# Cross-attention on one core: where seven of 16 transposed context tiles land in PSUM, in what order they are issued, and which slots split self-attention's weights

## The chip, the cores and the metric

The kernel runs on one core of a Trainium2 chip. The metric is the device time of one execution in microseconds (us), the median of the runs of one kernel. TensorE (PE), VectorE (DVE), ScalarE (ACT), GpSimd (POOL) and the DMA queue of SyncE (SP) each follow a list of instructions of their own and meet at semaphores.

## The reference, cut to what matters

```python
x = x + xattn(layernorm(x), ctx)      # x 4 x 128 x 512, ctx 4 x 2048 x 512, 16 heads of 32
x = x + self_attn(layernorm(x))       # 4 x 128 tokens, rotary, 16 heads
x = x + moe(layernorm(x))             # 8 experts, top 2, hidden 1024
# xattn:
cn = layer_norm(ctx, g2, b2)
k, v = cn @ Wk.T, cn @ Wv.T
out = softmax(q @ k.T / sqrt(32) + mask) @ v
return out @ Wo.T + bo
```

The change lies in the cross-attention, and in the preparation of self-attention's weights that is done beside it.

## The kernel before, in words

**Windows and slots.** The cross-attention goes through 16 windows, w = 4b + g, for batch b and a group g of four heads. A window has eight slots, p = 0 to 7, and a slot takes two tiles of 128 keys. `window_steps` (L57) writes the order of the steps of a window out by hand; `all_steps` (L154) puts the windows in a row behind a set-up, and every engine runs through the same list and takes its own part of each step. Only DVE's list is changed a little by `halves_behind_maxima` (L163): the subtraction of a block of keys is put behind the next two maxima or tiles.

**The steps of a slot.** PE has one long block per slot, in four pieces between which the other steps stand. Slot 0 is the last keys block of window w + 1 (`k`, L799), slots 1 to 4 are its four blocks of values (`v`, L815), and slots 5 to 7 are the first three blocks of keys of window w + 2. Around them stand:

- `s` (L854): the scores of the next slot, into `ps_s`; ACT takes the exponential of them (L694), POOL adds that to a running sum (L430).
- `av` (L869): the slot's probabilities times values.
- `p1` (L832): one of 16 products of queries and keys of window w + 1, of which DVE takes the maximum (L536). `MAXIMA_AT` (L52) says how many a slot holds: 2, 4, 4, 3 and 3 in slots 2 to 6. `mt` (L849) turns the maxima into a row.
- `st`, `nm`: DVE's statistics and normalisation of the next batch's context tiles, in windows with g below 3.
- `t` (L779), only in the windows with g = 2 of batches 0 to 2 (w = 2, 6 and 10, the turning windows): 16 context tiles of the next batch are transposed, four 128x128 transposes each. ACT copies the high half out of the bank (L630), DVE writes the rest as a low half (L524), and only then is the bank free. `TURNING_AT` (L54) gives the order of tiles and maxima in each slot, here `tptptp` in slots 2 to 5, `tptp` in 6 and `tt` in 7. The first four of a slot's such steps go between the four pieces of the long block, the fifth and the sixth behind it, ahead of `av`.
- `den`, `low`, `op`, `wo`: the end of the window before, and the output projection.

**Banks.** Two rings of two PSUM banks each serve these steps. Ring a (`ps_a`, `bank_a_free` L715) is for the blocks of keys and values and the output projection; of its two banks one is being filled while the one before is emptied by ACT. Ring b (`ps_b`, `bank_b_free` L728) is for `t`, `p1` and `mt`, which take its two banks in turn in the order of the steps. PE waits ahead of a step until the bank's last user has been read: for a `t` on DVE's low half (`tr_lo`), for a `p1` on its maximum (`p1_max`), for a block on ACT's copy (`k_f_out`, `v_out`).

**Self-attention's weights.** When the context tiles of the last batch are transposed, the four weights of self-attention are loaded into their place (`self_weight_in`, L315) as 16 pieces of 128x512. Each is split into two halves, `spl`: ACT writes the high half (L710), waiting for the low half of the piece before, and DVE then the low half (L586), waiting for ACT. `SPLITS_AT` (L53) puts five pieces into each of windows 11, 12 and 13 and the last into window 14: one in slot 0, two in slot 1, two in slot 7, all behind the third piece of the long block. Nothing in the cross-attention waits for them.

SP follows the same list. At every fourth `t` it waits until the tile is transposed and issues the next 1 MB load; at the second and the fourth block of keys it moves 12 parts of the halves into `k_stack`. After the 16 windows come self-attention and the mixture of experts, which the change does not touch.

Of the kernel before, what the change touches and what calls it, by code (L numbers as in the profile page):

```python
# [14 lines left out]
ALU, ACT, AX = mybir.AluOpType, mybir.ActivationFunctionType, mybir.AxisListType  # L15
# [36 lines left out]
MAXIMA_AT = {2: 2, 3: 4, 4: 4, 5: 3, 6: 3}  # L52
SPLITS_AT = {0: (0,), 1: (1, 2), 7: (3, 4)}  # L53
TURNING_AT = ("", "ppp", "tptptp", "tptptp", "tptptp", "tptptp", "tptp", "tt")  # L54


def window_steps(w):  # L57
# [11 lines left out]
    for p in range(NPAIR):  # L69
# [103 lines left out]


NORMED = ((0, NB - 1), (NB - 1, NB))

# [12 lines left out]
def cross_attention(nc, io, t, s):  # L189


    steps = all_steps("PE")
    ring_a = [step[:3] for step in steps if step[0] in ("k", "v", "op") and step[-1] == 0]
    ring_b = [step for step in steps if step[0] in ("t", "p1", "mt")]
    ring_a = [(step[0], step[1]) if step[0] == "op" else step for step in ring_a]
    KIN = 16 * 3 * HPG
# [6 lines left out]
    with ExitStack() as ctx:  # L203
# [94 lines left out]

        def bank_a(step):
            return ps_a[ring_a.index(step) % 2]  # L300

        def bank_b(step):
            return ps_b[ring_b.index(step) % 2]

# [137 lines left out]
        def _(v):  # L442
# [58 lines left out]
            for step in all_steps("DVE"):  # L501
# [19 lines left out]
                elif kind == "t":  # L521
                    b, kt = step[1:]
                    v.wait_ge(tr_hi, NKT * b + kt + 1)
                    nc.vector.tensor_tensor(cT_lo[:, :, P * kt:P * (kt + 1)],  # L524
                                            bank_b(step)[:, :].rearrange("p (c n) -> p c n", c=NC),
                                            cT_hi[:, :, P * kt:P * (kt + 1)], ALU.subtract).then_inc(tr_lo, 1)
# [6 lines left out]
                elif kind == "p1":  # L533
                    w, j, kb = step[1:]
                    v.wait_ge(p1_mm, nth_p1(step))
                    nc.vector.tensor_reduce(mpart[:, j, kb:kb + 1], bank_b(step)[:, :], AX.X, ALU.max).then_inc(p1_max, 1)  # L536
                    if (j, kb) == (HPG - 1, NKB - 1):
# [15 lines left out]
                elif kind == "op" and step[2] == NG - 1:  # L553
                    b = step[1]
                    v.wait_ge(op_mm, b + 1)
                    nc.vector.scalar_tensor_tensor(out=t.x[:, b, :], in0=bank_a(step[:2])[:, :], scalar=UNSCALE,
                                                   in1=t.x[:, b, :], op0=ALU.mult, op1=ALU.add).then_inc(x_done, 1)
# [17 lines left out]
                elif kind == "xln":  # L575
                    v.wait_ge(x_done, NB - 1)
                    for b in range(NB - 1):
                        nc.vector.bn_stats(t.a_stats[:, b, :], t.x[:, b, :]).then_inc(s.a_st, 1)
                    v.wait_ge(s.a_st, NB - 1)
                    for b in range(NB - 1):  # L580
                        last = nc.vector.bn_aggr(t.a_mv[:, b, :], t.a_stats[:, b, :])
                    last.then_inc(s.a_var, 1)
                elif kind == "spl":
                    n = step[1]
                    v.wait_ge(s.self_hi, n + 1)
                    nc.vector.scalar_tensor_tensor(out=self_weight(n, "lo"), in0=self_weight(n, "raw"),  # L586
                                                   scalar=W_SCALE, in1=self_weight(n, "hi"), op0=ALU.mult,
                                                   op1=ALU.subtract).then_inc(s.self_lo, 1)

        @block.scalar  # L590
        def _(act):
# [33 lines left out]
            for step in all_steps("ACT"):  # L625
                kind = step[0]
                if kind == "t":
                    b, kt = step[1:]
                    act.wait_ge(tr, NKT * b + kt + 1)
                    nc.scalar.activation(cT_hi[:, :, P * kt:P * (kt + 1)],  # L630
                                         bank_b(step)[:, :].rearrange("p (c n) -> p c n", c=NC),
                                         ACT.Copy).then_inc(tr_hi, 1)
# [13 lines left out]
                elif kind == "v" and step[3] == QUAD - 1:  # L646
                    w, q = step[1:3]
                    act.wait_ge(v_mm, NQ * w + q + 1)
                    if w == 0 and q == 0:
                        act.wait_ge(w_lo, 3)  # L650
                    nc.scalar.activation(vals[w % 2][:, QUAD * q:QUAD * (q + 1), :].rearrange("p k n -> p (k n)"),
                                         bank_a(step[:3])[:, :], ACT.Copy, scale=UNSCALE).then_inc(v_out, 1)
                elif kind == "k" and step[3] == NC - 1:
# [6 lines left out]
                    else:  # L660
                        act.wait_ge(q_lo_s, NG)
                    nc.scalar.activation(k_f[:, kb % 2, :], bank_a(step[:3])[:, :], ACT.Identity,
                                         bias=kbias[:, g:g + 1], scale=UNSCALE).then_inc(k_f_out, 1)
# [12 lines left out]
                elif kind == "mt":  # L676
# [4 lines left out]
                        t.q_stack[SHIFT_ROW:SHIFT_ROW + 1, HPG * g:HPG * (g + 1), b * P:(b + 1) * P],  # L681
                        bank_b(step)[SHIFT_ROW:SHIFT_ROW + 1, :].rearrange("o (j n) -> o j n", j=HPG),
                        ACT.Copy, scale=-1.0).then_inc(m_row, 1)
# [17 lines left out]
                elif kind == "wo":  # L701
                    c = step[1]
                    act.wait_ge(w_in[3], 16)
                    nc.scalar.activation(wo_hi[:, c, :], folded[3][1][:, c, :], ACT.Copy, scale=W_SCALE).then_inc(w_hi, 1)
                elif kind == "spl":
                    n = step[1]
# [7 lines left out]
        def _(pe):  # L714
            def bank_a_free(step):  # L715

                at = ring_a.index(step)
                if at >= 2:
                    before = ring_a[at - 2]
                    if before[0] == "k":  # L720
                        pe.wait_ge(k_f_out, NKB * before[1] + before[2] + 1)
                    elif before[0] == "v":
                        pe.wait_ge(v_out, NQ * before[1] + before[2] + 1)
                    else:
                        pe.wait_ge(x_done, before[1] + 1)
                return ps_a[at % 2]

            def bank_b_free(step):  # L728

                at = ring_b.index(step)  # L730
                if at >= 2:
                    before = ring_b[at - 2]
                    if before[0] == "t":
                        pe.wait_ge(tr_lo, NKT * before[1] + before[2] + 1)
                    elif before[0] == "p1":
                        pe.wait_ge(p1_max, nth_p1(before))
                    else:
                        pe.wait_ge(m_row, before[1] + 1)
                return ps_b[at % 2]

# [36 lines left out]
            for step in steps:  # L777
                kind = step[0]
                if kind == "t":  # L779
                    b, kt = step[1:]  # L780
                    bank = bank_b_free(step)
                    pe.wait_ge(normed, NKT * b + kt + 1)
# [16 lines left out]
                elif kind == "k":  # L799
                    w, kb, c = step[1:]  # L800
                    b, g = w // NG, w % NG
                    if c == 0:
                        bank_a_free(step[:3])
# [4 lines left out]
                    bank, col, keys = bank_a(step[:3]), slice(P * g, P * (g + 1)), slice(KB * kb, KB * (kb + 1))  # L808
                    nc.tensor.matmul(bank[:, :], t.wk_hi[:, c, col], cT_hi[:, c, keys], start=(c == 0), stop=False)  # L809
# [5 lines left out]
                elif kind == "v":  # L815
                    w, q, i = step[1:]
                    b, g = w // NG, w % NG
                    if i == 0:
                        bank_a_free(step[:3])
# [5 lines left out]
                    to, keys = bank_a(step[:3])[:, P * i:P * (i + 1)], slice(P * kt, P * (kt + 1))  # L825
                    for c in range(NC):
# [5 lines left out]
                elif kind == "p1":  # L832
                    w, j, kb = step[1:]
                    b, g = w // NG, w % NG
                    bank = bank_b_free(step)
                    if (j, kb) == (0, 0):
# [9 lines left out]
                elif kind == "mt":  # L846
                    w = step[1]
                    bank = bank_b_free(step)
                    pe.wait_ge(m_max, w + 1)  # L849
# [48 lines left out]
                elif kind == "op":  # L898
                    b, g = step[1:]
                    if g == 0:  # L900
                        bank_a_free(step[:2])
                        pe.wait_ge(w_lo, 3 + NC)
                    to = bank_a(step[:2])
                    pe.wait_ge(split_lo, NG * b + g + 1)
# [1070 lines left out]
```

## Time and profile before

| | us |
|---|---|
| runs | 1005.8, 1005.98, 1001.48 |
| median | 1005.8 |
| the profiled execution, its own time | 1000.39 |
| its span in the trace | 998.6 |
| mean granted TensorE clock in it | 0.959 of full speed |

The profiled execution is one more run. Its own time is 1.8 us above its span, and it lies 5.4 us below the median of the three. In the trace the windows' stage goes from 98 to about 664 us; in it the shown duration of a matmul is longer than the distance to the next, so times on PE are read here from start to start. A slot is measured from the start of one `av` (L879) to the start of the next.

### The profile page before, as it was taken

Reading aid. Unit: us, or ns where it says so; the run is one execution under the profiler, and the core shown is the slowest. Engines: PE = TensorE matmul, PEld = TensorE weight load, DVE = VectorE, ACT = ScalarE, POOL = GpSimd, SP = SyncE. Lnnn points to the kernel's source line nnn. Section 1 sums busy time; section 2 is a strip of 40 time slices with the busy share of each in tenths; the row PEclk is TensorE's granted clock in tenths of the full one; section 3 lists DMA queues with packets and bytes.
Section 4 is the critical chain, followed back from the end, with each engine's and each line's share of the span. In section 5 each row is a group of like instructions: output and inputs, shape, how many; then the busy total and the mean of one; then the engine's idle time right before and its main releaser. Section 6 shows DMA issues by size and latency. Waiting matters only on the chain. (4 is left out here: it accounts for less than half of the span.)

```text
span 998.6 us, 24592 instructions
## 1 busy us (share of the span) xinstructions
PE 908.0 (91%) x10413; PEld 609.7 (61%) x10413; DVE 687.8 (69%) x1024; ACT 529.6 (53%) x813; POOL 385.4 (39%) x290
## 2 busy tenths in 40 slices
PE   5998999999999999999999999996876669999996
PEld 2463775765765766766757657663444367777773
DVE  7764787646777645688546656665687757999993
ACT  3643345555344453444464544551376447999993
POOL 2130665344566435556435444452230132112112
PEclk9997999999999999999999999998897778999998
DMA  9362121352121332221332201216502727999993
GB/s 341 103 182 57 34 65 43 107 148 71 41 65 34 113 107 55 60 54 26 94 117 77 66 20 47 59 30 252 192 2 84 283 84 268 397 404 401 402 359 48
DMA packets 48456, 134.64 MB, mean 135 GB/s; under 512 B 9870, under 2 KB 11790, under 8 KB 44506
## 3 DMA queue, kind: packets, MB, share of 16 engines
q1 hardware_dynamic: 45356, 126.78, 37.6%
q0 software_dynamic: 2800, 6.04, 3.0%
q8 instruction: 83, 1.36, 0.6%
q10 hardware_dynamic: 192, 0.26, 0.1%
q14 instruction: 25, 0.20, 0.1%
HBM read 94.99 MB, written 11.33 MB: 106 GB/s over the span
## 5 line engine op out<-in xcount | busy, mean ns | idle before, releaser
L430 POOL TENSOR_TENSOR acc_pool<-acc_pool,pT 128x1024 f32<-128x1024 f32 x90 | 211.5, 2350 | 162.6 <-ACT pT L694 161.0
L536 DVE TENSOR_REDUCE mpart<-ps_b 128x1 f32<-128x512 f32 x256 | 174.0, 686 | 87.4 <-PE ps_b L843 86.5
L694 ACT ACTIVATE pT<-ps_s 128x1024 f32<-128x1024 f32 x124 | 126.5, 1021 | 199.3 <-PE ps_s L865 199.3
L827 PE MATMUL ps_a<-wv_hi,cT_hi 128*128 128x128 f16 x1024 | 184.3, 220 | 0.4 <-ACT kbias L611 0.4
L829 PE MATMUL ps_a<-wv_hi,cT_lo 128*128 128x128 f16 x1024 | 183.2, 219 | 0.0
L828 PE MATMUL ps_a<-wv_lo,cT_hi 128*128 128x128 f16 x1024 | 183.1, 219 | 0.0
L827 PEld LDWEIGHTS ps_a<-wv_hi,cT_hi 128*128 128x128 f16 x1024 | 99.8, 97 | 12.4 <-issue 11.9
L843 PE MATMUL ps_b<-k_stack,q_stack 98*128 98x512 f16 x256 | 98.0, 386 | 9.4 <-DVE mpart L536 5.4
L828 PEld LDWEIGHTS ps_a<-wv_lo,cT_hi 128*128 128x128 f16 x1024 | 100.2, 98 | 5.0
L531 DVE TENSOR_TENSOR k_lo<-k_f,k_hi 128x512 f16<-128x512 f32 x64 | 67.9, 1061 | 48.9 <-ACT k_hi L667 48.5
L829 PEld LDWEIGHTS ps_a<-wv_hi,cT_lo 128*128 128x128 f16 x1024 | 99.8, 97 | 0.0
L809 PE MATMUL ps_a<-cT_hi,wk_hi 128*128 128x512 f16 x256 | 98.3, 384 | 0.0
L865 PE MATMUL ps_s<-q_stack,k_stack 98*128 98x128 f16 x992 | 93.4, 220 | 5.3 <-ACT pT L694 4.3
L810 PE MATMUL ps_a<-cT_lo,wk_hi 128*128 128x512 f16 x256 | 97.3, 380 | 0.0
L811 PE MATMUL ps_a<-cT_hi,wk_lo 128*128 128x512 f16 x256 | 97.1, 379 | 0.0
L865 PEld LDWEIGHTS ps_s<-q_stack,k_stack 98*128 98x128 f16 x992 | 70.7, 98 | 40.9 <-ACT pT L694 11.0
L1846 PE MATMUL ps_h<-m_xT_hi,cT_hi 128*128 128x128 f16 x480 | 82.6, 221 | 2.4 <-issue 1.5
L1552 POOL DMA_INDIRECT out<-x_sb,rows_in x15 | 31.7, 2114 | 136.5 <-DMA out<-x_sb,rows_in 115.9
L879 PE MATMUL ps_o<-pT,vals 128*32 128x128 f32 x2048 | 82.4, 278 | 1.3 <-ACT pT L694 1.3
L1848 PE MATMUL ps_h<-m_xT_hi,cT_lo 128*128 128x128 f16 x480 | 82.5, 221 | 1.0 <-issue 1.0
L1847 PE MATMUL ps_h<-m_xT_lo,cT_hi 128*128 128x128 f16 x480 | 82.5, 221 | 0.1
L524 DVE TENSOR_TENSOR cT_lo<-ps_b,cT_hi 128x512 f16<-128x512 f32 x64 | 43.8, 689 | 52.7 <-ACT cT_hi L630 52.7
(255 smaller groups left out, 1877.7 us busy)
## 6 DMA issues: line engine op xcount, KB each, us to landing
w_raw<-in_w SPq DMA_DIRECT2D x30, 2048.0 KB, 12.9
raw<-in_context SPq DMA_DIRECT2D x16, 1024.0 KB, 5.8
k_stack<-k_hi SPq DMA_DIRECT2D x252, 64.0 KB, 2.0
k_stack<-k_lo SPq DMA_DIRECT2D x128, 64.0 KB, 2.0
slots_in<-a_zeros SPq DMA_DIRECT2D x1, 3855.0 KB, 12.8
rows_in<-slots_in SPq DMA_DIRECT2D x15, 257.0 KB, 11.6
q_stack<-k_stack SPq DMA_DIRECT2D x12, 128.0 KB, 2.3
x_sb<-in_x SPq DMA_DIRECT2D x2, 512.0 KB, 4.3
```

The lines of the kernel that those rows point to most:

```text
L430: nc.gpsimd.tensor_tensor(acc_pool[:, :], pT[:, 0, :] if p == 1 else acc_pool[:, :], pT[:, p % PT, :], ALU.add).then_inc(pool_add, 1)
L536: nc.vector.tensor_reduce(mpart[:, j, kb:kb + 1], bank_b(step)[:, :], AX.X, ALU.max).then_inc(p1_max, 1)
L694: nc.scalar.activation(pT[:, p % PT, :], scores(w, p)[:, :], ACT.Exp, scale=SM_SCALE).then_inc(exp_done, 1)
L809: nc.tensor.matmul(bank[:, :], t.wk_hi[:, c, col], cT_hi[:, c, keys], start=(c == 0), stop=False)
L810: nc.tensor.matmul(bank[:, :], t.wk_hi[:, c, col], cT_lo[:, c, keys], start=False, stop=False)
L811: last = nc.tensor.matmul(bank[:, :], t.wk_lo[:, c, col], cT_hi[:, c, keys], start=False, stop=(c == NC - 1))
L827: nc.tensor.matmul(to, cT_hi[:, c, keys], t.wv_hi[:, c, col], start=(c == 0), stop=False)
L828: nc.tensor.matmul(to, cT_hi[:, c, keys], t.wv_lo[:, c, col], start=False, stop=False)
L829: last = nc.tensor.matmul(to, cT_lo[:, c, keys], t.wv_hi[:, c, col], start=False, stop=(c == NC - 1))
L843: nc.tensor.matmul(bank[:, :], t.q_stack[0:ROWS, HPG * g + j, b * P:(b + 1) * P], t.k_stack[w % 2][0:ROWS, j, KB * kb:KB * (kb + 1)], star ...
L865: last = nc.tensor.matmul(scores(w, p)[:, at:at + P], t.k_stack[w % 2][0:ROWS, j, P * kt:P * (kt + 1)], t.q_stack[0:ROWS, HPG * g + j, b * ...
L1846: nc.tensor.matmul(to, w1_hi[u][:, c, col], xT_hi[u][:, c, :], start=(c == 0), stop=False)
```

## The change

Four things are edited. (1) Seven of the 16 tiles of batches 1 to 3, those in `ASIDE`, go into a bank of ring a instead of ring b: the one whose turn comes next, while the current block fills the other. The other nine tiles, the `p1` and the `mt` keep ring b. `banks_of` notes for each use its bank and the use before it in that bank, and PE waits for that. (2) The order of tiles and maxima in the turning windows' slots 3, 4 and 6 is another. (3) In a slot, a fifth such step stands behind `den`, `low` and `op`, right ahead of `av`, and a sixth behind `av`. (4) Self-attention's pieces: one a slot, in the same windows; ACT's high half is in slots 1 to 5, DVE's low half one slot later, in 2 to 6, behind the slot's second maximum.

```diff
-SPLITS_AT = {0: (0,), 1: (1, 2), 7: (3, 4)}
-TURNING_AT = ("", "ppp", "tptptp", "tptptp", "tptptp", "tptptp", "tptp", "tt")
+TURNING_AT = ("", "ppp", "tptptp", "ttppt", "tptppt", "tptptp", "tpptp", "tt")
+
+ASIDE = (0, 4, 6, 7, 10, 12, 15)
...
-        behind = [("spl", 5 * (w - 11) + n) for n in SPLITS_AT.get(p, ()) if 11 <= w and 5 * (w - 11) + n < 4 * NC]
...
-        for n in range(max(4, len(side))):
+        low, high = [[("spl" + part, 5 * (w - 11) + q - 2)] if w >= 11 and 2 <= q <= 6 and 5 * (w - 11) + q - 2 < 4 * NC
+                     else [] for part, q in (("_lo", p), ("_hi", p + 1))]
+        for n in range(4):
             steps += heavy[n:n + 1] + side[n:n + 1]
             if n == 1:
-                steps += nxt[:1] + light[:1]
+                steps += nxt[:1] + low + light[:1]
             if n == 2:
-                steps += nxt[1:] + light[1:] + behind
+                steps += nxt[1:] + high + light[1:]
+        late = [side[4:5], side[5:6]]
...
-        steps += [("av", w, p, 0), ("av", w, p, 1)]
+        steps += late[0] + [("av", w, p, 0), ("av", w, p, 1)] + late[1]
...
+def banks_of(steps):
+
+    begun, last, place = {"a": 0, "b": 0}, {}, {}
+    for step in steps:
+        kind = step[0]
+        use = step[:2] if kind == "op" else step[:3]
+        if kind in ("k", "v", "op"):
+            if use in place:
+                continue
+            bank = ("a", begun["a"] % 2)
+            begun["a"] += 1
+        elif kind == "t" and step[1] and step[2] in ASIDE:
+            bank = ("a", begun["a"] % 2)
+        elif kind in ("t", "p1", "mt"):
+            use = step
+            bank = ("b", begun["b"] % 2)
+            begun["b"] += 1
+        else:
+            continue
+        place[use] = (bank, last.get(bank))
+        last[bank] = use
+    return place
...
-            def bank_b_free(step):
-
-                at = ring_b.index(step)
-                if at >= 2:
-                    before = ring_b[at - 2]
-                    if before[0] == "t":
-                        pe.wait_ge(tr_lo, NKT * before[1] + before[2] + 1)
...
+            def bank_free(use):
+
+                before = banks[use][1]
+                if before is not None and before[0] == "k":
+                    pe.wait_ge(k_f_out, NKB * before[1] + before[2] + 1)
...
+                elif before is not None and before[0] == "t":
+                    pe.wait_ge(tr_lo, NKT * before[1] + before[2] + 1)
...
+                return bank_at(use)
```

The order of PE in slots 2 to 6 of a turning window after the change, with V and K for a piece of the long block, t for a tile, t* for a tile in ring a, p for a maximum's product and s for scores:

```
slot 2   V t0* V p s V t1  s V p      t2  av
slot 3 p V t3  V t4* s V p s V p      t5  av
slot 4   V t6* V p s V t7* s V p      p   av
slot 5 t8 K t9 K p s K t10* s K p     t11 av
slot 6 p K t12* K p s K p  s K        t13 av
```

Slot 7 has `mt`, t14 and t15*. The step ahead of slot 3, 5 and 6 is the sixth of the slot before.

## Rows read from the trace of the kernel before

**Rows 1.** The page: busy time of the engines over the span.

```profile
PE 908.0 (91%) x10413; PEld 609.7 (61%) x10413; DVE 687.8 (69%) x1024; ACT 529.6 (53%) x813; POOL 385.4 (39%) x290
```

**Rows 2.** Windows view: stretch, length, busy us of PE, PEld, DVE, ACT, POOL, clock.

```profile
137.37:141.59 4.22, 4.22 (x82) 3.68 (x73) 4.14 (x11) 1.67 (x4) 3.48 (x4) 1.00 0.34 81
141.59:146.28 4.69, 4.69 (x79) 3.86 (x77) 3.42 (x10) 1.74 (x3) 2.78 (x4) 1.00 0.29 70
150.96:155.34 4.38, 4.38 (x41) 2.20 (x40) 3.32 (x9) 1.28 (x3) 2.49 (x2) 1.00 0.00 0
173.92:180.31 6.39, 6.09 (x95) 5.01 (x86) 4.48 (x8) 3.83 (x8) 2.99 (x2) 1.00 0.38 92
193.16:199.50 6.34, 6.02 (x53) 3.50 (x52) 3.87 (x6) 3.23 (x6) 2.35 (x2) 1.00 0.34 130
...
173.92:204.92 31.00, 29.46 (x365) 21.38 (x356) 19.83 (x34) 15.75 (x27) 11.76 (x5) 1.00 0.39 122
482.62:513.64 31.02, 29.48 (x366) 21.40 (x358) 19.84 (x34) 15.77 (x27) 11.78 (x5) 1.00 0.38 118
...
399.48:403.75 4.27, 4.27 (x46) 2.27 (x45) 1.29 (x2) 2.77 (x4) 0.30 (x1) 1.00 0.44 110
531.41:537.17 5.76, 4.85 (x78) 3.86 (x76) 4.99 (x9) 2.82 (x5) 2.35 (x1) 1.00 0.21 51
554.95:560.72 5.77, 4.34 (x45) 2.27 (x44) 2.24 (x3) 3.40 (x5) 0.31 (x1) 1.00 0.42 102
```

**Rows 3.** Waits of PE from 80 to 660 us: total us, times, longest.

```profile
PE ps_b L843 <- DVE mpart L536: 5.2, 10, 0.9
PE ps_b L784 <- DVE cT_lo L524: 4.6, 15, 0.3
PE ps_s L865 <- ACT pT L694: 4.3, 3, 1.4
```

**Rows 4.** Timeline of PE in slot 2 of window 2: start, us, instruction, [idle].

```profile
177.37 0.61 PE L784 MATMUL ps_b<-ident_sb,raw 128*128 128x128 f32 x4
177.82 0.39 PE L865 MATMUL ps_s<-q_stack,k_stack 98*128 98x128 f16 x4
178.71 0.38 PE L843 MATMUL ps_b<-k_stack,q_stack 98*128 98x512 f16 x1
179.39 0.66 PE L784 MATMUL ps_b<-ident_sb,raw 128*128 128x128 f32 x4 [0.30 <-DVE cT_lo L524]
179.99 0.39 PE L843 MATMUL ps_b<-k_stack,q_stack 98*128 98x512 f16 x1
```

**Rows 5.** Timeline of ACT and DVE in slots 2 and 5 of window 2.

```profile
178.02 0.60 ACT L630 ACTIVATE cT_hi<-ps_b 128x512 f16<-128x512 f32 x1 [1.63 <-PE ps_b L784]
...
197.70 1.02 ACT L694 ACTIVATE pT<-ps_s 128x1024 f32<-128x1024 f32 x1
198.60 0.69 ACT L662 ACTIVATE k_f<-ps_a,kbias 128x512 f32<-128x512 f32 x1
...
199.86 0.58 ACT L630 ACTIVATE cT_hi<-ps_b 128x512 f16<-128x512 f32 x1
...
178.65 0.69 DVE L524 TENSOR_TENSOR cT_lo<-ps_b,cT_hi 128x512 f16<-128x512 f32 x1 [0.48 <-ACT cT_hi L630]
```

**Rows 6.** Timeline of POOL and DVE in window 11, slots 1 and 3 to 4.

```profile
527.54 2.35 POOL L430 TENSOR_TENSOR acc_pool<-acc_pool,pT 128x1024 f32<-128x1024 f32 x1 [1.44 <-ACT pT L694]
...
537.56 2.35 POOL L430 TENSOR_TENSOR acc_pool<-acc_pool,pT 128x1024 f32<-128x1024 f32 x1 [0.64 <-ACT pT L694]
...
527.95 2.49 DVE L586 SCALAR_TENSOR_TENSOR parts<-raw,parts 128x512 f16<-128x512 f32 x1 [0.69 <-ACT parts L710]
...
539.74 0.69 DVE L536 TENSOR_REDUCE mpart<-ps_b 128x1 f32<-128x512 f32 x1 [0.20 <-PE ps_b L843]
```

**Rows 7.** Windows view of the windows' stage and of all behind it.

```profile
98.00:662.00 564.00, 548.50 (x7098) 375.05 (x7096) 370.28 (x599) 271.07 (x389) 298.56 (x193) 1.00 0.25 68
662.00:998.60 336.60, 279.64 (x2816) 190.68 (x2813) 252.71 (x293) 218.80 (x357) 70.69 (x60) 0.90 0.64 236
```

More of the change, by code:

```diff
@@ L192, in cross_attention @@
     steps = all_steps("PE")
-    ring_a = [step[:3] for step in steps if step[0] in ("k", "v", "op") and step[-1] == 0]
-    ring_b = [step for step in steps if step[0] in ("t", "p1", "mt")]
-    ring_a = [(step[0], step[1]) if step[0] == "op" else step for step in ring_a]
+    banks = banks_of(steps)
     KIN = 16 * 3 * HPG
@@ L297, in scores, with bank_at @@
             return ps_bb if w == WINDOWS - 1 and p % 2 else ps_s
[L299 to L303, printed above, removed]
+        def bank_at(use):
+            ring, n = banks[use][0]
+            return (ps_a if ring == "a" else ps_b)[n]
         block = ctx.enter_context(nc.Block())
@@ L651, in _ @@
                     nc.scalar.activation(vals[w % 2][:, QUAD * q:QUAD * (q + 1), :].rearrange("p k n -> p (k n)"),
-                                         bank_a(step[:3])[:, :], ACT.Copy, scale=UNSCALE).then_inc(v_out, 1)
+                                         bank_at(step[:3])[:, :], ACT.Copy, scale=UNSCALE).then_inc(v_out, 1)
                 elif kind == "k" and step[3] == NC - 1:
@@ L661, in _ @@
                         act.wait_ge(q_lo_s, NG)
-                    nc.scalar.activation(k_f[:, kb % 2, :], bank_a(step[:3])[:, :], ACT.Identity,
+                    nc.scalar.activation(k_f[:, kb % 2, :], bank_at(step[:3])[:, :], ACT.Identity,
                                          bias=kbias[:, g:g + 1], scale=UNSCALE).then_inc(k_f_out, 1)
@@ L714, in _ @@
         def _(pe):
-            def bank_a_free(step):
-                at = ring_a.index(step)
-                if at >= 2:
[L719 to L726, printed above, removed]
-            def bank_b_free(step):
-                at = ring_b.index(step)
-                if at >= 2:
-                    before = ring_b[at - 2]
-                    if before[0] == "t":
-                        pe.wait_ge(tr_lo, NKT * before[1] + before[2] + 1)
[L735 to L739, printed above, removed]
+            def bank_free(use):
+                before = banks[use][1]
+                if before is not None and before[0] == "k":
+                    pe.wait_ge(k_f_out, NKB * before[1] + before[2] + 1)
+                elif before is not None and before[0] == "v":
+                    pe.wait_ge(v_out, NQ * before[1] + before[2] + 1)
+                elif before is not None and before[0] == "op":
+                    pe.wait_ge(x_done, before[1] + 1)
+                elif before is not None and before[0] == "t":
+                    pe.wait_ge(tr_lo, NKT * before[1] + before[2] + 1)
+                elif before is not None and before[0] == "p1":
+                    pe.wait_ge(p1_max, nth_p1(before))
+                elif before is not None and before[0] == "mt":
+                    pe.wait_ge(m_row, before[1] + 1)
+                return bank_at(use)
             def bias_in_a_row(i):
@@ L780, in _ @@
                     b, kt = step[1:]
-                    bank = bank_b_free(step)
+                    bank = bank_free(step)
                     pe.wait_ge(normed, NKT * b + kt + 1)
@@ L802, in _ @@
                     if c == 0:
-                        bank_a_free(step[:3])
+                        bank_free(step[:3])
                         pe.wait_ge(tr_lo, NKT * b + QUAD * (kb + 1))
@@ L807, in _ @@
                             pe.wait_ge(bias_out, 3)
-                    bank, col, keys = bank_a(step[:3]), slice(P * g, P * (g + 1)), slice(KB * kb, KB * (kb + 1))
+                    bank, col, keys = bank_at(step[:3]), slice(P * g, P * (g + 1)), slice(KB * kb, KB * (kb + 1))
                     nc.tensor.matmul(bank[:, :], t.wk_hi[:, c, col], cT_hi[:, c, keys], start=(c == 0), stop=False)
@@ L818, in _ @@
                     if i == 0:
-                        bank_a_free(step[:3])
+                        bank_free(step[:3])
                         pe.wait_ge(tr_lo, NKT * b + QUAD * (q + 1))
@@ L824, in _ @@
                     kt, col = QUAD * q + i, slice(P * g, P * (g + 1))
-                    to, keys = bank_a(step[:3])[:, P * i:P * (i + 1)], slice(P * kt, P * (kt + 1))
+                    to, keys = bank_at(step[:3])[:, P * i:P * (i + 1)], slice(P * kt, P * (kt + 1))
                     for c in range(NC):
@@ L834, in _ @@
                     b, g = w // NG, w % NG
-                    bank = bank_b_free(step)
+                    bank = bank_free(step)
                     if (j, kb) == (0, 0):
@@ L847, in _ @@
                     w = step[1]
-                    bank = bank_b_free(step)
+                    bank = bank_free(step)
                     pe.wait_ge(m_max, w + 1)
```

18 lines of the change are left out of this document (9 added, 9 removed).

## The prediction

> **What bounds the kernel now.** The page first: PE is busy 91% of the span and no other engine over 69% [rows 1], so a stall of PE in the windows' stage is paid in full, and one of another engine is not. Second, the windows view cuts that stage into slots. An undisturbed slot with a values block and four maxima takes 4.69 us, one with two maxima 4.22, so a maximum costs (4.69 - 4.22)/2 = 0.23; one with a keys block and three maxima takes 4.38 [rows 2]. Third, the timeline of PE in a turning window: a tile's four transposes take 0.45, from 177.37 to the scores at 177.82 [rows 4]. From these prices the same work can be summed without stalls. Slots 2 to 6 of a turning window hold three values blocks, two keys blocks, 13 maxima and 14 tiles: slots 2, 3 and 4 would be 4.69 - 0.23 + 3 x 0.445 = 5.79 each, slot 5 4.38 + 1.33 = 5.71, slot 6 (one maximum, two tiles) 4.38 - 0.46 + 0.89 = 4.81, together 27.9. They take 31.0 in window 2 and the same in window 10 [rows 2], so **3.1 us of stalls in each of three turning windows**, some 0.6 in each slot: slot 2 takes 6.39, slot 5 6.34.
>
> The waits view names them: 15 waits of a tile's transposes on DVE's low half, five a window [rows 3]. The timeline shows one. The maximum's product starts at 178.71, the third tile could follow 0.22 later, at 178.93, and starts at 179.39: 0.46 lost. Its own product of the next maximum starts after 0.60 in place of 0.44, at 179.99: 0.16 more [rows 4]. The reason is the turn of a bank. The tile that began at 177.37 is copied by ACT from 178.02, its low half starts at 178.65 and takes 0.69 [rows 5], and PE has the bank at 179.39: 2.02 us, whereas ring b of two banks asks for it after 1.56.
>
> The same view gives the splits' price. Slot 3 of window 11 takes 5.76 in place of 4.69, and the step from slot 7 to the next window's slot 0 takes 5.77 in place of 4.27 [rows 2]. Each comes three times: the waits view has three of scores on ACT's exponential, 4.3 us, and those of the first maxima on DVE among ten [rows 3]. **1.07 x 3 + 1.50 x 3 = 7.7 us.**
>
> **The change, part by part.**
>
> *Banks and order of the tiles.* No instruction is added or removed: 16 tiles, 16 maxima, the same copies and subtractions, so the 27.9 stay, only dealt otherwise (5.55, 5.79, 5.36, 5.93, 5.27 for slots 2 to 6). I walk the new order with these prices, a bank being free 2.0 after a tile's start and a maximum's 1.3 after its own (178.71 to 179.99 [rows 4]).
> - Slot 2: t1 and t2 still lie in one bank of ring b with nothing between them but scores, a piece and a product. t2 waits as now, 0.46. The product behind it now stands behind `av`, so its 0.16 goes.
> - Slot 3: t3 is in t2's bank and comes some 1.95 after it, 0.07 late. t4 is in ring a, whose last block ACT emptied long before; t5 follows a maximum begun 1.3 before.
> - Slot 4: t6 and t7 share a bank of ring a, 2.2 apart: free by 0.2.
> - Slot 5: its block of keys wants t7's bank 3.1 after it; free. t8 wants a bank whose maximum stands in DVE's queue behind t7's low half, which ACT gives late in the slot: 0.16.
> - Slot 6: t11's high half stands on ACT behind the exponential (1.02) and the keys' pair of copies (198.60 to 199.86, 1.26 [rows 5]). The second product of slot 6 wants its bank: 0.24, and the two behind it some 0.1 each, 0.46 in all. Now that place costs 0.6.
> - Slot 7 and the next slot 0: the last block of keys wants t15's bank 2.2 after its start, with the subtraction of a keys block between: just free, by less than 0.1.
>
> Sum 0.46 + 0.07 + 0.16 + 0.46 = 1.15 in place of 3.1: **1.95 a window, 5.9 us in three.** No row shows a tile in ring a, so the bounds: at worst only the 0.16 behind each of four tiles goes (0.6 a window, 1.9 in all, if every other wait returns elsewhere), at best all 3.1 x 3 = 9.3. The walked value lies between.
>
> Queues that steps are moved past. SP: the loads hang on every fourth tile, which moves by under 2 us and later not at all; what they fill is read a batch later. Both batches of `k_stack` parts are used from slot 2 of the next window on; the subtraction ahead of the second comes earlier, behind t14 and not t15. The one DMA wait of a turning window, in slot 1, hangs on the window before and stays. POOL: its adds follow the exponentials, one of 2.35 us a slot [rows 6] against slots of 5 to 6 us. ACT and DVE: their own work is under 20 of 31 us [rows 2]; only its order matters, as walked.
>
> *The pieces of weights.* Sixteen splits remain. Those in slots 0, 1 and 7, where DVE waits for ACT's high half in the same slot and ACT for the last low half, ahead of the exponential, go: the 7.7 us. What covers them in slots 2 to 6: on DVE a low half alone takes 0.69 (the maxima's time); between the second maximum's end and the third's start DVE is idle for about 0.4, so the third comes 0.2 to 0.3 late, and its bank is wanted two products later, over 1 us on. On ACT the high half stands behind the exponential, 0.63 ahead of the copy of the block, whose bank is wanted a slot later. In slot 6 the last maximum is 0.6 late and `mt`, a piece of block later, has 0.4 left. Cost taken: 0; if that cover were gone, a piece costs up to 1.07, what slot 3 shows now. In slot 2 of window 14 one piece stands ahead of statistics, no one waiting.
>
> A rule speaks against this place. The row first: the piece at 527.95 took 2.49 and ended 0.55 after POOL's add (527.54 + 2.35 = 529.89) [rows 6], and every slot from 2 to 6 has such an add. But the add of slot 4 begins at 537.56 and ends at 539.91, and the second maximum begins at 539.74 and holds DVE until 540.4 [rows 6]; the piece comes 0.4 behind the add. I take no collision. The Trainium skill, SBUF — State Buffer, section on the rules for kernel authors, states it: a DVE instruction with two SBUF inputs and a GpSimd one that reads SBUF exclude each other, and the later blocks fully until the first ends. By that rule the trace agrees at 527.95, and a piece in each of these slots would meet an add; it is a rival below.
>
> **Sum.** 5.9 + 7.7 = 13.6 us. Against the profiled execution 1000.4 - 13.6 = 986.8; against the median of the three runs, 5.4 above it, 1005.8 - 13.6 = **992.2**. I forecast the median; a set of runs near the profiled one would lie some 4 us lower, as one of three did.
>
> **The rivals.**
> 1. *The tiles gain nothing.* Each stall is a chain through three engines; if the walk is a few tenths short at ACT, the waits only move to products and blocks. For it: the margins of 0.1 and 0.2 above. Against: the long gaps, 3 us, for most tiles in ring a. 1005.8 - 7.7 = 998.1.
> 2. *The clock gives it back.* In the windows' stage the granted clock is 1.00, behind it 0.90 [rows 7], so some 67 of 336 us are at 1.2 and not 2.4 GHz there. A shift of 14 us may fall on the spells otherwise: 20 us more at the lower level, half of it lost, leave -3.6: 1002.2, within 0.5%. For it: runs of one kernel 4.5 us apart. Against: the change touches nothing there.
> 3. *Pieces meet POOL's adds,* by the rule above. Sixteen pieces at up to 1.07 cost 17.1 in place of 7.7: +9.4 - 5.9 = +3.5, 1009.3. It decides if the add ends later than the second maximum, 0.4 us off.
> 4. *Slower: the long blocks wait for tiles.* Now a block in ring a waits for one copy of ACT. After it, seven tiles a batch put ACT and DVE, in order, ahead of a block or of the next tile. If exponential and keys' pair (1.02 + 1.26 = 2.28) came ahead of every one, the margins I walked (over 2 for t0 and t12, 1.7, 0.2, 1.1, 0.8, 0.2 for the others) leave 0.6 + 2.1 + 1.2 + 1.5 + 2.1 = 7.5 a window, 22.5 in three: +8.9, 1014.7. It decides once ACT's copy of a tile in ring a comes over 1 us after PE has it. For it: ACT's idle time does not order its queue. Against: at 178.02 and in all of slot 4 the copy goes first.
>
> **How the numbers follow.** Forecast 0.69, rivals 0.14, 0.06, 0.06, 0.05. The forecast spans 992.2 with 4 us either way for its tiles and 4 more downwards for the level of the runs; with rival 1's 998.1 that is 986 to 999, 0.8 of the chance. Measured on this kernel, 0.5%, 5 us, is about what can be told from no change. Faster by more: forecast and rival 1, 0.83. Within it: rivals 2 and 3, 0.12. Slower: 0.05.
>
> **What would show it.** In the changed profile: slots 2 to 6 of window 2 at 29.0 and not 31.0 us, with five waits on low halves down to two or three; slot 3 of windows 11 to 13 at 4.7 and the slot 0 after them at 4.3; no wait of scores on the exponential; L586 at 0.69 each, nowhere 2.49; clock 1.00 up to the end of window 14. Waits of L809 or L827 on DVE's low half would mean rival 4, pieces of 2 us rival 3. The forecast is wrong if the three turning windows give back under 3 us, or if the splits' six stalls turn up at other lines.

## The result, and the profile after

The changed kernel takes 994.9 us in the median of six runs (986.7 to 998.5), the kernel before 1001.6 (999.5 to 1006.0, the three shown ahead among them). The ratio is 0.991, 95% interval 0.988 to 0.994. In a second set of six runs it was 990.6 against 1002.5, ratio 0.988 (0.985 to 0.991). The ratios compare means. So it is faster, by 0.9 and 1.2%, 9 and 12 us; the medians of the first set are 6.7 apart, those of the second 11.9. The forecast was 13.6.

The page after, the line that answers to [rows 1]:

```profile
PE 904.5 (91%) x10413; PEld 608.5 (61%) x10413; DVE 681.9 (68%) x1024; ACT 529.5 (53%) x813; POOL 386.5 (39%) x290
```

The waits of PE from 80 to 660 us after (total us, times, longest), which answer to [rows 3]; L859 is the maxima's product (L843 before), L800 a tile's transposes (L784):

```profile
PE ps_b L800 <- DVE cT_lo L549: 4.5, 6, 1.2
PE ps_b L859 <- DMA k_stack<-k_lo: 3.6, 3, 1.7
PE ps_b L859 <- DVE mpart L561: 2.9, 9, 0.8
```

Scores no longer wait for the exponential, and the maxima's products lost the three long waits of the splits, 0.91 each (the 0.8 that is left lies ahead of window 0, at 84 us, and was there before). Tiles wait six times and not 15, but for the same 4.5 us: the longest is 1.2 and not 0.3.

The windows view after: slots 2 to 6 of window 2 one by one, all five together, slot 3 of window 11, slot 0 of window 12, and windows 11 to 13 from `av` to `av`. They answer to [rows 2].

```profile
175.22:181.28 6.06, 5.76 (x94) 4.92 (x86) 4.53 (x9) 3.56 (x7) 2.67 (x2) 1.00 0.40 97
181.28:188.50 7.22, 6.00 (x89) 5.09 (x88) 5.71 (x7) 3.05 (x6) 2.11 (x2) 1.00 0.27 101
188.50:193.85 5.35, 5.35 (x85) 4.59 (x84) 2.94 (x5) 2.60 (x5) 2.30 (x1) 1.00 0.24 71
193.85:199.97 6.12, 6.01 (x55) 4.01 (x54) 4.06 (x8) 3.39 (x7) 2.35 (x1) 1.00 0.47 168
199.97:205.55 5.58, 5.58 (x48) 2.96 (x47) 4.19 (x8) 3.51 (x7) 2.35 (x1) 1.00 0.54 191
175.22:205.55 30.33, 28.71 (x365) 21.56 (x356) 21.43 (x33) 16.12 (x27) 11.78 (x5) 1.00 0.38 125
531.58:536.26 4.68, 4.68 (x79) 3.85 (x77) 2.58 (x4) 2.25 (x4) 2.36 (x1) 1.00 0.28 66
554.03:558.31 4.28, 4.28 (x45) 2.28 (x45) 0.69 (x1) 2.77 (x4) 0.32 (x1) 1.00 0.42 102
523.29:630.94 107.65, 107.65 (x1405) 72.52 (x1404) 61.33 (x88) 55.70 (x82) 54.22 (x24) 1.00 0.21 55
```

Windows 11 to 13 have PE busy for all of their 107.65 us; with the pieces in their old places they take 115.36 (second experiment), so the pieces gave 7.7. Slots 2, 4 and 5 of the turning window are where they were forecast, to 0.05, and slot 6 is 0.15 below. Slot 3 is not: 7.22 us where the walk said 5.86, more than any slot of that window before. Its reason is in the timeline of slots 2 and 3 of window 2: DVE, POOL, PE.

```profile
180.56 0.68 DVE L561 TENSOR_REDUCE mpart<-ps_b 128x1 f32<-128x512 f32 x1
181.15 2.32 DVE L576 SCALAR_TENSOR_TENSOR oT_lo<-oT,vbias,oT_hi 128x128 f16<-128x128 f32 x1
183.40 0.68 DVE L549 TENSOR_TENSOR cT_lo<-ps_b,cT_hi 128x512 f16<-128x512 f32 x1
...
180.97 2.36 POOL L455 TENSOR_TENSOR acc_pool<-acc_pool,pT 128x1024 f32<-128x1024 f32 x1 [3.04 <-ACT pT L719]
...
180.69 0.66 PE L800 MATMUL ps_b<-ident_sb,raw 128*128 128x128 f32 x4 [0.30 <-DVE cT_lo L549]
184.13 0.65 PE L800 MATMUL ps_b<-ident_sb,raw 128*128 128x128 f32 x4 [1.22 <-DVE cT_lo L549]
```

The instruction at 181.15 is the step `low`, the small low half of the window before's output (128x128; in the windows that do not turn 0.32 to 0.35 us, and 0.59 in windows 4 and 8). It took 2.32 us: POOL's add had begun at 180.97, ended at 183.33, and `low` ended 0.14 behind it. Behind `low` in DVE's queue stood the third tile's low half, started at 183.40 although ACT had the high half by 181.99; and the fourth tile, in the same bank, waited 1.2 us for it. Before the change `low` stood behind the two steps that slot 2 then issued ahead of `av`, and started 0.11 before the add's end:

```profile
179.67 2.36 POOL L430 TENSOR_TENSOR acc_pool<-acc_pool,pT 128x1024 f32<-128x1024 f32 x1 [3.04 <-ACT pT L694]
...
181.92 0.34 DVE L551 SCALAR_TENSOR_TENSOR oT_lo<-oT,vbias,oT_hi 128x128 f16<-128x128 f32 x1
```

Edit (3) moved the fifth step behind `den` and `low` and the sixth behind `av`, and so `low` ahead of both on DVE, into the add.

The sum of the stage, from the first `av` of window 0 to that of window 14: 540.1 us before (98.38 to 638.50), 531.3 after (99.66 to 630.94), 8.8 less. That is 7.7 for the pieces and 3 x 0.67 = 2.0 for the tiles, less 0.9 by which slot 1 of the turning windows, with its wait on a DMA, was longer in this execution.

The profiled execution took 998.5, the slowest of its six; its span is only 2.0 shorter than before. The windows began 1.3 later, the stretch between them and the mixture was 2.1 shorter, and the mixture 7.9 longer, from the first to the last product of L1844 (L1828 before). The view of that line gives count, durations and first and last start: before, after, and the same kernel profiled once more (`e11_changed_again`).

```profile
L1828 PE MATMUL ps_y<-parts,h_hi x120: 377/379/634, 832.3 to 990.4; 128*128 128x512 f16 x120
```

```profile
L1844 PE MATMUL ps_y<-parts,h_hi x120: 376/379/634, 822.6 to 988.6; 128*128 128x512 f16 x120
```

```profile
L1844 PE MATMUL ps_y<-parts,h_hi x120: 376/379/634, 823.2 to 981.0; 128*128 128x512 f16 x120
```

158.1, 166.0 and 157.8 us. In the first profiled execution of the changed kernel ACT waited 14.7 us for the experts' weights, before 5.6, in the repeat 5.4. SP's issues of the mixture's loads of first weights (count, durations, first and last start), in the same order:

```profile
L1505 SPq DMA_DIRECT2D w_raw<-in_w x11: 328/333/430, 834.2 to 945.7; - x11
```

```profile
L1521 SPq DMA_DIRECT2D w_raw<-in_w x11: 327/333/430, 830.6 to 944.0; - x11
```

```profile
L1521 SPq DMA_DIRECT2D w_raw<-in_w x11: 328/333/430, 825.0 to 936.3; - x11
```

The first of them is issued 1.9, 8.0 and 1.8 us after PE's first product there. Those 8 us are in the execution, since first and repeat are one kernel; more on them below.

### The profile page after: what moved, and what is told of

The parts are those of the page before. It is cut to its first block and busy times, and to the rows that moved or that the text cites. A ratio compares the mean times of both kernels' runs of the same rounds, so it can differ in the third digit from the quotient of the medians.

```text
span 996.6 us, 24592 instructions
## 1 busy us (share of the span) xinstructions
PE 904.5 (91%) x10413; PEld 608.5 (61%) x10413; DVE 681.9 (68%) x1024; ACT 529.5 (53%) x813; POOL 386.5 (39%) x290
## 5 line engine op out<-in xcount | busy, mean ns | idle before, releaser
L843 PE MATMUL ps_a<-wv_hi,cT_hi 128*128 128x128 f16 x1024 | 184.3, 220 | 0.4 <-ACT kbias L636 0.4
L556 DVE TENSOR_TENSOR k_lo<-k_f,k_hi 128x512 f16<-128x512 f32 x64 | 72.3, 1129 | 69.9 <-ACT k_hi L692 69.9
L843 PEld LDWEIGHTS ps_a<-wv_hi,cT_hi 128*128 128x128 f16 x1024 | 99.8, 97 | 11.8 <-issue 11.3
L859 PE MATMUL ps_b<-k_stack,q_stack 98*128 98x512 f16 x256 | 96.8, 384 | 8.2 <-DMA k_stack<-k_lo 5.3
L1568 POOL DMA_INDIRECT out<-x_sb,rows_in x15 | 30.3, 2020 | 141.7 <-DMA out<-x_sb,rows_in 111.4
L895 PEld LDWEIGHTS ps_o<-pT,vals 128*32 128x32 f32 x2048 | 49.7, 109 | 36.5 <-issue 32.0
```

Source lines behind the costliest of these rows:

```text
L843: nc.tensor.matmul(to, cT_hi[:, c, keys], t.wv_hi[:, c, col], start=(c == 0), stop=False)
L859: nc.tensor.matmul(bank[:, :], t.q_stack[0:ROWS, HPG * g + j, b * P:(b + 1) * P], t.k_stack[w % 2][0:ROWS, j, KB * kb:KB * (kb + 1)], star ...
L895: last = nc.tensor.matmul(ps_o[w % 2][HD * j:HD * (j + 1), 0:P], vals[w % 2][:, 2 * p + i, HD * j:HD * (j + 1)], pT[:, p % PT, at:at + P], ...
```

## The experiments

**One part alone.** `e1_splits_only` is the kernel before with edit (4) alone, `e2_tiles_only` the changed kernel with the pieces in their old places.

> The kernel before with the pieces of weights alone moved. Theory: the change's gain is almost all here. Windows 11 to 13, from av to av, go from 37.6 + 40.2 + 37.6 = 115.4 us to 107.7, slot 3 from 5.76 to 4.69 and slot 0 of the next window from 5.77 to 4.27; no wait of scores on ACT's exponential is left; the windows' stage is 7.7 us shorter and the time over the rounds 0.992 of before. The turning windows keep 31.0 us in slots 2 to 6. Rival (the pieces meet POOL's adds): pieces of 2 us and over, 115 us or more. Rival (the stage behind gives it back): the windows' stage is shorter but the ratio is 1.00.

> The changed kernel with the old places of the pieces of weights. Theory: the tiles' part is worth 0.7 us a turning window: slots 2 to 6 take 30.3 us in place of 31.0, with slot 3 at 7.2, since the low half of the window before's output (0.34 us alone) meets POOL's add and holds the third tile; in three windows 2.0 us, ratio 0.998. Windows 11 to 13 keep 115.4 us. Rival (the tiles' part is worth what was forecast and something else took it in the changed kernel): slots 2 to 6 at 29.0, ratio 0.994.

Windows view, the first kernel: windows 11 to 13, and slots 2 to 6 of window 2.

```profile
524.43:632.08 107.65, 107.65 (x1406) 72.53 (x1405) 61.31 (x88) 55.64 (x82) 54.19 (x24) 1.00 0.21 55
175.06:206.06 31.00, 29.46 (x365) 21.38 (x356) 19.82 (x34) 15.76 (x27) 11.77 (x5) 1.00 0.39 122
```

The same stretches of the second:

```profile
523.04:638.40 115.36, 108.37 (x1405) 72.52 (x1404) 71.96 (x88) 56.30 (x82) 54.15 (x24) 1.00 0.20 53
175.23:205.57 30.34, 28.72 (x366) 21.56 (x358) 21.44 (x33) 16.13 (x27) 11.78 (x5) 1.00 0.39 125
```

The parts don't touch each other: 7.7 and 3 x 0.66 us in the traces. Ratios 0.991 (0.988 to 0.994) and 0.998 (0.996 to 1.000), as expected. The runs alone would not tell the pieces alone from the whole change, 0.991 both; the traces do.

**The instruction in the way.** `e3_low_behind` moves `low`:

```diff
-        if w and p == 2:
-            steps.append(("low", w - 1))
...
         steps += late[0] + [("av", w, p, 0), ("av", w, p, 1)] + late[1]
+        if w and p == 2:
+            steps.append(("low", w - 1))
```

> The changed kernel with one DVE instruction moved: the low half of the window before's output stands behind the slot's last step, as DVE had it before, and no longer ahead of the third tile's low half. Theory (it blocks on POOL's add there and holds the tile): slot 3 of a turning window goes from 7.22 to 5.9 us, slots 2 to 6 from 30.3 to 29.0, 4.0 us in three windows; the fourth tile waits 0.1 and not 1.2 us; ratio to before 0.987. Rival (the tile waits on ACT's copy, which is behind the exponential and the values' copy): slot 3 stays at 7.2.

The timeline of DVE in slots 2 and 3 of window 2, and the windows view of slot 3 and of slots 2 to 6:

```profile
181.94 0.69 DVE L549 TENSOR_TENSOR cT_lo<-ps_b,cT_hi 128x512 f16<-128x512 f32 x1 [0.78 <-ACT cT_hi L655]
182.54 0.68 DVE L561 TENSOR_REDUCE mpart<-ps_b 128x1 f32<-128x512 f32 x1
183.14 0.34 DVE L576 SCALAR_TENSOR_TENSOR oT_lo<-oT,vbias,oT_hi 128x128 f16<-128x128 f32 x1
```

```profile
181.20:187.05 5.85, 5.85 (x89) 5.09 (x88) 3.87 (x7) 3.06 (x6) 2.10 (x2) 1.00 0.41 124
175.14:204.09 28.95, 28.55 (x365) 21.55 (x356) 19.53 (x33) 16.11 (x27) 11.77 (x5) 1.00 0.41 129
```

`low` takes 0.34 at the end of the add, slot 3 5.85 and the five slots 28.95; the forecast's walk had given 5.86 and, added up, 29.05. The ratio is 0.986 (0.982 to 0.989).

Is it its place or POOL? `e4_short_add` leaves every instruction where the change has it and shortens the add. It leaves out seven eighths of that one sum.

```diff
+                    n = P if w in (2, 6, 10) and p == 3 else 2 * KB
-                    nc.gpsimd.tensor_tensor(acc_pool[:, :], ...
+                    nc.gpsimd.tensor_tensor(acc_pool[:, 0:n], ...
```

> The changed kernel, but POOL's add of the fourth exponential of windows 2, 6 and 10 takes 128 of its 1024 columns; the rest of that sum is left out. Nothing else is moved. Theory (the low half of the window before's output blocks on this add, nothing else in its place is wrong): it takes 0.34 us and not 2.32, slot 3 falls from 7.22 to 5.9 us, slots 2 to 6 to 29.0, as with the instruction moved. Rival (its place ahead of the third tile costs by the order alone, whatever POOL does): slot 3 stays over 6.5.

The timeline of POOL and DVE in slot 2 of window 2, and slot 3 in the windows view:

```profile
180.53 0.46 POOL L456 TENSOR_TENSOR acc_pool<-acc_pool,pT 128x128 f32<-128x128 f32 x1 [3.04 <-ACT pT L720]
...
180.71 0.42 DVE L577 SCALAR_TENSOR_TENSOR oT_lo<-oT,vbias,oT_hi 128x128 f16<-128x128 f32 x1
```

```profile
180.83:186.68 5.85, 5.85 (x88) 5.08 (x87) 3.90 (x7) 3.06 (x6) 0.21 (x2) 1.00 0.46 119
```

With `low` where it was and the add short, the 1.37 us are gone. The add is the cause, the place only what brings `low` into it. It is not any DVE instruction that an add holds up. `low` reads two tiles in SBUF; a tile's low half reads one, and the other input is in PSUM. Of the 48 low halves of tiles in the windows of the changed kernel, 15 start under an add, and all 15 take 0.69. One of them, in slot 4 of window 2:

```profile
188.44 2.36 POOL L455 TENSOR_TENSOR acc_pool<-acc_pool,pT 128x1024 f32<-128x1024 f32 x1 [5.11 <-ACT pT L719]
...
189.31 0.69 DVE L549 TENSOR_TENSOR cT_lo<-ps_b,cT_hi 128x512 f16<-128x512 f32 x1 [0.45 <-ACT cT_hi L655]
```

**The other place of a piece.** The forecast let the pieces go free by a margin of 0.4 us behind the add. `e8_piece_first` takes the margin away: DVE's low half stands at the start of its slot.

```diff
+        steps += low
         for n in range(4):
...
-                steps += nxt[:1] + low + light[:1]
+                steps += nxt[:1] + light[:1]
```

> The changed kernel with DVE's low half of each piece at the start of its slot, ahead of the first maximum, where POOL's add of 2.35 us runs. Theory (the place behind the second maximum costs nothing because the add is over by then, by 0.4 us): here each of the 15 pieces of windows 11 to 13 waits the add out, takes 2 us or more, holds the maxima by 0.7 to 1.1, and windows 11 to 13 take 118 to 124 us in place of 107.7. Rival (a piece fits anywhere in the slot, since the maxima have slack): 108.

POOL and DVE in slot 3 of window 11, PE's wait, and the windows view of that slot and of windows 11 to 13:

```profile
533.40 2.35 POOL L456 TENSOR_TENSOR acc_pool<-acc_pool,pT 128x1024 f32<-128x1024 f32 x1 [2.12 <-ACT pT L720]
...
533.81 2.49 DVE L612 SCALAR_TENSOR_TENSOR parts<-raw,parts 128x512 f16<-128x512 f32 x1 [0.52 <-ACT parts L736]
...
536.96 0.39 PE L860 MATMUL ps_b<-k_stack,q_stack 98*128 98x512 f16 x1 [0.74 <-DVE mpart L562]
```

```profile
532.80:538.39 5.59, 4.85 (x79) 3.86 (x77) 4.77 (x6) 2.25 (x4) 2.35 (x1) 1.00 0.21 51
524.51:641.46 116.95, 109.53 (x1405) 72.14 (x1404) 82.96 (x88) 55.63 (x82) 54.17 (x24) 1.00 0.19 50
```

The piece ends at 536.30, 0.55 behind the add (535.75), as the piece at 527.95 had [rows 6]. Windows 11 to 13 take 9.3 us more than with the change, 1.6 more than with the old places; I had expected 10 to 16, since I took every slot to lose. Slot 2 lost nothing (4.23 in all three windows), whose piece starts 1.1 us into the add and takes 1.81, and nor did slot 5 of window 12, whose piece meets none (0.68). The rival of the forecast was right in its mechanism; in the change's place for the pieces it does not come about.

**Ring a and the order.** `e6_ring_b_only` sets `ASIDE = ()`, `e7_old_order` keeps the seven tiles in ring a and restores the old `TURNING_AT`.

> The changed kernel with no tile in ring a: all 16 take the two banks of ring b in turn, in the new order. Theory (the second ring is what the order lives on): pairs of tiles come 1.1 us apart in banks that are free after 2, so slots 3 to 6 stall more than before the change, slots 2 to 6 take 32 us or more against 30.3 with ring a and 31.0 before. Rival (the order does it and the ring is idle decoration): 30.3.

> The changed kernel with the seven tiles in ring a and the old order of tiles and maxima. Theory (ring a takes the pressure off, the order is fine tuning): slots 2 to 6 take 30.3 us within 0.5, slot 3 is again over 7 with the same blocked instruction; without that instruction's 1.3 it would be 29. Rival (without the new order tiles in ring a meet each other or the next block): over 31.0, with waits of the long blocks on DVE's low halves.

Slots 2 to 6 of window 2 in the windows view, of the one and the other:

```profile
175.37:206.94 31.57, 29.00 (x366) 21.57 (x357) 21.77 (x33) 15.98 (x27) 11.79 (x5) 1.00 0.36 120
```

```profile
175.32:205.75 30.43, 28.72 (x365) 21.60 (x357) 21.59 (x34) 15.55 (x27) 11.77 (x5) 1.00 0.40 124
```

Both have the 1.37 of `low` in slot 3 (7.22 each). Ring a is worth 31.57 - 30.33 = 1.2 us a window, less than the 1.7 or more that I had expected; the new order, with ring a, 0.1. Without ring a the rest of the change is slower than the kernel before (31.0), and only because of the 1.37. No run has edit (3) alone. These two kernels, `e4_short_add` and `e8_piece_first` have one run each; what is said of them is read from their traces.

**Slot 2.** `e5_low_and_order` adds to the third experiment the order `ttpptp` in slot 2.

> As the one before, and slot 2's order of tiles and maxima is ttpptp in place of tptptp, so that two products and not one lie between the second and the third tile, and they lie in different banks of ring b. Theory: the third tile's wait of 0.46 goes, slot 2 takes 5.6 and not 6.06 us, slots 2 to 6 28.6, another 1.3 us in three windows; ratio 0.986. Rival: the wait moves to the product or the tile at the start of slot 3, which gets longer by the same 0.4, and the sum stays at 29.0.

Slot 2 and slots 2 to 6 of window 2 in the windows view:

```profile
175.19:181.19 6.00, 5.76 (x94) 4.92 (x86) 4.49 (x8) 3.72 (x7) 2.86 (x2) 1.00 0.38 93
175.19:204.09 28.90, 28.55 (x365) 21.55 (x357) 19.54 (x33) 16.23 (x27) 11.80 (x5) 1.00 0.42 130
```

A miss: 0.05 us and not 0.45 a window. The third tile no longer waits for a tile's low half but for a maximum, three times in all, since between the second tile's low half and that maximum DVE also normalises a tile. Ratio 0.986 (0.983 to 0.989), the same as without it.

**Why runs of one kernel differ.** `e9_light_before` and `e10_light_after` load only half of the experts' weights from the mixture's first loads on, in the kernel before and in the changed one; the other half is what lay there.

```diff
-                sp.dma_start(w1_raw[k % 2][:, :, :], weights_of(io.w1, k))
+                sp.dma_start(w1_raw[k % 2][:, 0:NC // 2, :], weights_of(io.w1, k)[:, 0:NC // 2, :])
```

(and so for w2)

> The kernel before, but from the third or fourth tile of the mixture on only half of each expert's weights is loaded; the other half is what lay there. Theory (the scatter between runs, and how much of the windows' gain a single run shows, come from the stream of the experts' weights, some 400 GB/s at the end): the runs lie within 3 us of each other, where the kernel before spans 9, and PE has no wait in the mixture for weights. Rival (the scatter is the clock's): it stays at 8 us or so.

> The changed kernel with the same half loads in the mixture. Theory: this is shorter than the one before by what the windows' stage gives, 9.7 us (7.7 of the pieces, 2.0 of the tiles) less up to 1 of DMA waits, with 3 us of scatter. Rival (the stage behind gives part of the gain back by itself, as the profiled execution of the changed kernel seemed to show with 5 of 9 us): the difference is 4 to 5 us here too.

The eight runs of the first lie between 990.4 and 996.5 (median 994.0), the four of the second between 981.0 and 985.0 (983.6): 10.4 us apart in the medians, so the gain of the windows comes through, and the rival's 4 to 5 do not. The scatter expectation failed for the kernel before: 6.1 us over eight runs against 7.4 of the full kernel beside it. There the longest run has a lower mean granted clock than the shortest: 996.5 at 0.962 and 990.4 at 0.969, 1004.3 at 0.962 and 996.9 at 0.971 in the full kernel. Over the 8 and the 11 runs the correlation of time and clock is -0.85 and -0.90; in the other sets it is weaker, -0.25 to -0.74.

What the loads cost shows in two traces whose PE comes to the mixture at nearly the same time, `e7_old_order` (full weights) and `e10_light_after`. SP's first issue and PE's products of the one, then of the other:

```profile
L1521 SPq DMA_DIRECT2D w_raw<-in_w x11: 327/333/1105, 822.9 to 934.2; - x11
L1844 PE MATMUL ps_y<-parts,h_hi x120: 376/379/379, 813.4 to 977.6; 128*128 128x512 f16 x120
```

```profile
L1521 SPq DMA_DIRECT2D w_raw<-in_w x11: 327/333/737, 823.3 to 927.5; - x11
L1844 PE MATMUL ps_y<-parts,h_hi x120: 376/379/379, 814.0 to 971.0; 128*128 128x512 f16 x120
```

In both PE is over 9 us ahead of the first load. With full weights it then needs 164.2 us and ACT waits 14.5 for them, with half of them 157.0 and no wait (and `e9_light_before`, with PE 9.5 ahead, 156.9). The profiles with full weights are all of one kind or the other. Where the first load is issued at most 2.0 us behind PE's first product (before, and six more: labels e1, e2, e3, e5, e11 and e12), the mixture takes 157.2 to 158.3. Where it comes 8.0 to 11.1 behind (after, and e4, e6, e7 and e8, which shared a chip), it takes 164.1 to 166.0. So PE that comes early, measured against its loads, gives 7 to 8 us back to them. Since one kernel shows both kinds (after and its repeat), this is no part of the change. What sets the distance was not tried. For the changed kernel the chain that ended last (start, us, by what) shows what its first load waited for, the records that POOL sends to `slots_in`, and that from there load, high half and low half follow each other five times up to 943.8:

```profile
818.54 5.76 DMA slots_in<-m_second,m_rows
...
830.63 12.08 DMA w_raw<-in_w
842.74 1.92 ACT cT_hi L1719
844.68 4.51 DVE cT_lo L1686 x2
849.21 16.48 DMA w_raw<-in_w
```

These loads are 8% of the span in that chain, and 9% in those of e4, e6 and e8. The kernel before, e1, e3 and e12 have none in theirs, which is PE at 18%.

**Side by side.** Last, the changed kernel and the one with `low` moved, on one chip.

> The changed kernel itself, side by side with the one after it on one chip. Theory (its first profiled execution lost some 8 us of the windows' gain in the mixture by a slow stream of weights, in that execution and not as a rule): the windows' stage is 8.8 us shorter than before, the mixture as long as before, and the ratio of the rounds is 0.991. Rival (an earlier start of the mixture costs the gain again): most executions have the longer mixture.

> The changed kernel with the low half of the window before's output behind the slot's last step, as once before, now side by side with the changed kernel. Theory: 4.1 us less than it, three times the 1.37 of slot 3, ratio to before 0.987. Rival: within the noise of the changed kernel, 0.991.

Medians 990.6 and 988.4, ratios 0.988 (0.985 to 0.991) and 0.987 (0.984 to 0.990). This pair alone does not separate them. Its traces do: slots 2 to 6 take 30.3 and 29.0 us in each turning window. With the first sets, 12 runs of each average 992.4 and 988.2, 4.2 apart, beside the 4.1 of the trace; that it fits so well is luck, since the two sets by themselves give 6.6 and 1.7. The kernel with `low` moved is the fastest version tried, with slot 2's new order or without.

## Why the prediction was right or wrong

**What bounds the kernel** held in the windows' stage: what PE stalled less there is what the stage got shorter. The prices (0.23 a maximum, 0.45 a tile) gave 27.9 for the work of slots 2 to 6; PE shows 28.7 busy after, in which matmuls are shown longer than their distance. That a stall there is "paid in full" did not hold in every execution: the mixture of the first profiled one gave back 7.9 of the 8.8, so that it took 998.5 and not the 986.8 of the forecast.

**The pieces of weights**, 7.7 forecast, 7.7 measured. Every one of the six stalls went and none came back elsewhere. L611 (L586 before) takes 0.68 on average over its 16, PE has no idle time in windows 11 to 13. The margin to the add, forecast at 0.4, is 0.2 in slot 3, where the add ends at 534.54 and the piece starts at 534.75, and 0.4 or more in the other slots.

**The tiles**, 5.9 forecast, 2.0 measured: the term that was mis-sized. Of its signs of being wrong the forecast named this one, under 3 us from the three turning windows. Step by step for a window: slot 2 6.01 forecast, 6.06 measured; slot 3 5.86 and 7.22; slot 4 5.36 and 5.35; slot 5 6.09 and 6.12; slot 6 5.73 and 5.58. The step that failed is "t3 is in t2's bank and comes some 1.95 after it, 0.07 late", and with it "ACT and DVE: their own work is under 20 of 31 us [rows 2]; only its order matters, as walked". I followed the tiles, the maxima and the copies past each other and left out that edit (3) also takes two of DVE's steps from ahead of `low` to behind it. Its own time, 0.34, would have been harmless. Beside the add it is 2.32. The rule I had cited, the Trainium skill, SBUF — State Buffer, section on the rules for kernel authors, is the rule that applies: `low` has two SBUF inputs as the piece has. The trace agrees in three places, 2.32 under an add of 2.36, 0.42 beside one of 0.46, 0.34 where the add is almost over. In the first two `low` ended 0.14 behind the add, in the third 0.23. I weighed it for the instruction that the change is about and not for the one that it pushes aside.

With that put right, in the third experiment, the walk is within 0.1 us of the trace, and the sum would have been 13.6: the stage is 14.1 shorter there (540.1 to 526.1), and the ratios of its two sets give 14.4 and 12.9 of 1002.

**The rivals.** The first, tiles that gain nothing, is nearest to the truth in size but not in kind: the tiles' waits on low halves did go, in slots 4 to 6. The second, the clock, did not come: behind the windows' stage the mean granted clock is 0.90 before (662.00 to 998.60) and 0.91 after (654.40 to 996.60). The third needs the piece in the add and was shown where it was put there. The fourth did not come: no long block waits on a low half.

**The median.** The 992.2 stood on a median of 1005.8 of three runs; over the six it is 1001.6, and the 994.9 after is 6.7 below that. That 992.2 and 994.9 lie close is thus in part luck, two errors of opposite sign: a gain 6.9 too large by the medians, of which the traces explain 3.9 and the scatter of the runs covers the rest, and a kernel before 4.2 too slow.

## What to carry to other kernels

When steps are moved past each other in a list that every engine follows, go through each engine's queue at that place, and list also the small steps that change their place only because others moved. A DVE instruction there with two SBUF inputs has two prices, its own and the rest of a POOL add that it may meet; here 0.34 and 2.3 us. Give what is queued behind it, and who waits for that, the second price. An instruction with one input in PSUM had no second price here.

## What had not been expected

- A 128x128 instruction of 0.34 us cost PE 1.4 us in each of three windows, two thirds of what the tiles' part could give (3 x 1.37 = 4.1 of 6.1 us).
- In the mixture PE's start says less of the end than the first load's issue does: in the 12 profiles with full weights the last product of L1844 (L1828) starts 153.5 to 158.4 us after the first load's issue, whether PE had begun 0.7 us after that issue or 11.1 before it.
- The mixture's time is thus of two sorts, 157 to 158 and 164 to 166 us, in different executions of one kernel. Two profiles that differ by 8 us there tell nothing of a change made elsewhere.
